# Sending the inverse RMS to all partitions through DRAM instead of through TensorE

## What is computed

```python
def _rmsnorm(x):
    return x * jax.lax.rsqrt(jnp.mean(x * x, axis=-1, keepdims=True) + EPS)

def _ada_rmsnorm(x, t, gamma_w, beta_w):
    gamma = (t @ gamma_w.T)[:, None, :]
    beta = (t @ beta_w.T)[:, None, :]
    return gamma * _rmsnorm(x) + beta

x = _L0_cond_ref(...)      # conditioned layer norm
x = x + a_alpha * _attention(_ada_rmsnorm(x, t, attn_gamma_w, attn_beta_w), W_q, W_k, W_v, W_o)
return x + f_alpha * _swiglu(_ada_rmsnorm(x, t, ffn_gamma_w, ffn_beta_w), gate_w, hidden_w, out_w, out_b)
```

## Time and profile before

| | |
|---|---|
| median of 3 runs | 1015.37 us (1011.99 to 1016.5) |
| profiled execution, its own time | 1012.19 us |
| span of its profile | 1010.4 us |
| busy PE / DVE / ACT / POOL | 964.5 / 691.4 / 625.8 / 565.9 us |
| granted TensorE clock, mean | 0.995 of full speed |

### The profile page before, as it was taken

How to read it: one execution, slowest core, us unless ns; L and a number is a source line. 1 busy time by engine, 2 the same in 40 slices (tenths; PEclk the granted TensorE clock), 3 DMA queues, 4 the chain that set the end, 5 groups by cost and what they waited for, 6 DMA issues and landing times.

```text
span 1010.4 us, 28503 instructions
## 1 busy us (share of the span) xinstructions
PE 964.5 (95%) x11164; PEld 900.0 (89%) x11164; DVE 691.4 (68%) x1347; ACT 625.8 (62%) x1775; POOL 565.9 (56%) x532
## 2 busy tenths in 40 slices
PE   5576999999999999999999999999999999999997
PEld 4455999999999999999999999999999999998897
DVE  6677676676777667677766767776777676666564
ACT  4556666667666666666666666666666666665432
POOL 4476646566564656656465665656565574443321
PEclk9899999999999999999999999999999999999999
DMA  6100001010100101010010101000000000000000
GB/s 209 43 22 22 2 12 33 12 33 2 33 13 12 33 12 33 2 33 12 12 33 13 32 2 34 12 13 32 13 25 9 13 12 13 12 13 12 12 12 21
DMA packets 20916, 23.36 MB, mean 23 GB/s; under 512 B 1200, under 2 KB 20272, under 8 KB 20784
## 3 DMA queue, kind: packets, MB, share of 16 engines
q1 hardware_dynamic: 20784, 21.54, 6.5%
HBM read 13.15 MB, written 8.39 MB: 21 GB/s over the span
## 4 chain that ended last, share of the span: by engine, by line
PE 86%; DVE 5%; issue 4%; ACT 3%; POOL 1%; DMA 0%; POOLq 0%; SPq 0%; ACTq 0%; DVEq 0%
PE psum L283 17%; PE psum L285 16%; PE psum L284 16%; PE psum L475 6%; PE psum L474 6%; PE psum L473 5%; PE psum L409 5%; PE psum L398 4%; PE psum L420 4%; PE psum L332 2%; PE psum L313 2%; ACT probs L826 2%; PE psum L321 1%; DVE least L585 1%; PE psum L469 1%
## 5 line engine op out<-in xcount | busy, mean ns | idle before, releaser
L283 PE MATMUL psum<-xf_hi,ffn_hi 128*128 128x256 f32 x1024 | 287.5, 281 | 4.2 <-DVE normed_f L633 1.6
L285 PE MATMUL psum<-xf_hi,ffn_lo 128*128 128x256 f32 x1024 | 285.9, 279 | 0.0
L284 PE MATMUL psum<-xf_lo,ffn_hi 128*128 128x256 f32 x1024 | 285.8, 279 | 0.0
L826 ACT ACTIVATE probs<-psum,least 128x64 f32<-128x64 f32 x976 | 213.0, 331 | 53.5 <-DVE least L585 30.0
L656 DVE SCALAR_TENSOR_TENSOR late<-tanh,psum 128x512 f32<-128x512 f32 x128 | 88.0, 687 | 188.7 <-ACT tanh L849 188.7
L283 PEld LDWEIGHTS psum<-xf_hi,ffn_hi 128*128 128x128 f32 x1024 | 192.2, 188 | 5.7 <-issue 4.4
L855 ACT ACTIVATE prod_hi<-late 128x512 fp32r<-128x512 f32 x128 | 80.7, 631 | 187.9 <-DVE late L664 129.0
L285 PEld LDWEIGHTS psum<-xf_hi,ffn_lo 128*128 128x128 f32 x1024 | 192.4, 188 | 0.0
L284 PEld LDWEIGHTS psum<-xf_lo,ffn_hi 128*128 128x128 f32 x1024 | 191.8, 187 | 0.0
L1006 POOL TENSOR_TENSOR probs<-probs,inv_sum 128x512 f32<-128x512 f32 x128 | 139.7, 1091 | 76.7 <-DVE inv_sum L606 76.2
L475 PE MATMUL psum<-prod_hi,ffn_lo 128*128 128x256 f32 x512 | 143.6, 281 | 0.0
(11 more groups left out here) (103 smaller groups left out, 2215.6 us busy)
## 6 DMA issues: line engine op xcount, KB each, us to landing
out_t_dram<-x_res SPq DMA_DIRECT2D x32, 256.0 KB, 2.1
xin<-x_dram SPq DMA_DIRECT2D x15, 512.0 KB, 3.9
w_raw<-attn_w_dram SPq DMA_DIRECT2D x1, 1024.0 KB, 7.0
x_res<-gate_w_dram SPq DMA_DIRECT2D x1, 1024.0 KB, 9.7
late<-hidden_w_dram SPq DMA_DIRECT2D x1, 1024.0 KB, 11.7
x_res<-out_w_dram SPq DMA_DIRECT2D x1, 1024.0 KB, 5.6
xin<-x_dram SPq DMA_DIRECT2D x2, 256.0 KB, 2.9
k_heads<-mod_w_dram SPq DMA_DIRECT2D x1, 320.0 KB, 4.6
```

Source lines behind the costliest of these rows:

```text
L283: pe.matmul(out, stat_hi, mov_hi, start=first, stop=False)
L284: pe.matmul(out, stat_hi, mov_lo, start=False, stop=False)
L285: return pe.matmul(out, stat_lo, mov_hi, start=False, stop=last)
L826: op = act.activation(probs[g % 2][:, h * SEQ:(h + 1) * SEQ], scores[:, h // 2, h % 2], ACT.Exp, bias=least[g % 2][:, h:h + 1], scale=-1.0)
```

## The change

The numbers `mean_sq` no longer go through TensorE in rounds with `grp >= 0`. SP writes them to a small DRAM tensor after GpSimd's power (second slot) and reads them back with the same row going to all 128 partitions, into `w_raw`, a tile that has served its time by then. The order of tokens in the transposes of the sums is changed so that the DRAM row is in token order. DVE's two scaling steps read `w_raw` (SBUF) where they read `norm_bank` (PSUM), and stand after `product` of the third slot. GpSimd's two beta steps move from the third slot into the fourth. ACT's two high parts move from before the exponentials of the fourth slot to between them and `half_tanh`. `ffn_split_lo` moves behind `product` of the fourth slot.

```diff
+        inv_dram = nc.dram_tensor("inv_dram", [2, 2 * PART], F32).ap()
+        inverse = [w_raw[:, i * 2 * PART:(i + 1) * 2 * PART] for i in range(2)]
...
+            def spread_inverses(grp):
+                which = slice(0 if is_part(grp + 2) else 1, 2 if is_part(grp - 2) else 1)
+                sp.wait_ge(inv_made, grp + 3)
+                sp.dma_start(inv_dram[grp % 2].rearrange("(w p i) -> p w i", w=2, i=2)[:, which],
+                             mean_sq[:].rearrange("p (w i) -> p w i", i=2)[:, which]).then_inc(inv_stored, 16)
...
+                sp.wait_ge(inv_stored, 16 * (grp + 1))
+                cols = slice(which.start * PART, which.stop * PART)
+                sp.dma_start(inverse[grp % 2][:, cols], inv_dram[grp % 2:grp % 2 + 1, cols].partition_broadcast(P)
+                             ).then_inc(spread_loaded, 16)
...
+                if s % PSEQ == 1 and s >= 0 and is_group(s // PSEQ):
+                    spread_inverses(s // PSEQ)
...
-                if norm_step(s) == 2 and is_group(grp) and s >= -4:
+                if norm_step(s) == 2 and -4 <= s < 0:
                     spread_inverses(grp)
...
-            def scale_by_rms(normed, first):
-                return dve.tensor_tensor(normed[:], normed[:],
-                                         norm_bank[:, first:first + PART].unsqueeze(1).broadcast_to([P, KT, PART]),
+            def scale_by_rms(normed, inverses):
+                return dve.tensor_tensor(normed[:], normed[:], inverses.unsqueeze(1).broadcast_to([P, KT, PART]),
                                          ALU.mult)
...
             def scale_f(m):
-                dve.wait_ge(inv_spread, m + 5)
                 dve.wait_ge(gamma_f, m + 1)
-                scale_by_rms(normed_f, PART).then_inc(scaled_f, 1)
+                dve.wait_ge(spread_loaded, 16 * (m + 3))
+                scale_by_rms(normed_f, inverse[m % 2][:, PART:2 * PART]).then_inc(scaled_f, 1)
```

More of the change, by code:

```diff
@@ L195, in norm_cols, with token_cols @@
             return slice(0 if is_part(grp + 2) else 2 * n, 4 * n if is_part(grp - 2) else 2 * n)
+        def token_cols(grp, ap, i):
+            return ap[:].rearrange("p (t i) -> p i t", i=2)[:, i] if grp >= 0 else ap[:, i * P:(i + 1) * P]
         def part_mod(row, m):
@@ L298, in norm_bank_read @@
                     pe.wait_ge(ms_read, grp + 3)
-                if j == 2 and is_part(grp + 2):
+                if j == 2 and grp < 0:
                     pe.wait_ge(scaled_a, grp + 3)
-                if j == 2 and is_part(grp - 2):
-                    pe.wait_ge(scaled_f, grp - 1)
             def norm_bank_free(s):
@@ L329, in spread_inverses @@
                 pe.wait_ge(inv_made, grp + 3)
-                cols = norm_cols(grp, 1)
-                for i in range(cols.start, cols.stop):
+                for i in range(2):
                     mm = pe.transpose(norm_bank[:, i * P:(i + 1) * P], mean_sq[:, i:i + 1].broadcast_to([P, P]),
@@ L623, in mean_squares_out @@
                 dve.wait_ge(ms_mm, grp + 3)
-                if grp >= -1:
+                if grp >= 1:
+                    dve.wait_ge(inv_stored, 16 * grp)
+                elif grp >= -1:
                     dve.wait_ge(inv_spread, grp + 2)
@@ L721, in _ @@
                     mean_squares_out(grp)
-                if norm_step(s) == 2 and is_part(grp + 2):
+                if norm_step(s) == 2 and s < 0:
                     scale_a(grp + 2)
@@ L753, in _ @@
                     product(f)
+                if j == 2 and s >= 0 and is_part(grp + 2):
+                    scale_a(grp + 2)
+                if j == 2 and is_part(grp - 2):
+                    scale_f(grp - 2)
+                if j == 3 and is_part(grp - 2):
+                    ffn_split_lo(grp - 2)
                 if grp % 2 == 0 and 2 <= (grp + 4) // 2 < NBLK:
@@ L900, in _ @@
                     attended_hi(grp - 1)
-                if j == 3 and is_part(grp + 2) and s != -1:
+                if s == FIRST_SLOT + 3:
                     split_hi_a(grp + 2)
-                if j == 3 and is_part(grp - 2):
-                    split_hi_f(grp - 2)
                 if s == FIRST_SLOT + 3:
@@ L911, in _ @@
                     exponentials(s)
+                if j == 3 and s >= 0 and is_part(grp + 2):
+                    split_hi_a(grp + 2)
+                if j == 3 and is_part(grp - 2):
+                    split_hi_f(grp - 2)
                 if is_step(f):
@@ L1038, in _ @@
                     inverse_rms(grp)
[L1039 removed]
+                if norm_step(s) == 2 and s < 0 or j == 3 and s >= 0 and is_part(grp + 2):
+                    apply_beta_a(grp + 2)
+                if j == 3 and is_part(grp - 2):
                     apply_beta_f(grp - 2)
[L1041 to L1042 removed]
                 if j == 3 and is_part(grp + 2) and s != -1:
```

23 lines of the change are left out of this document (15 added, 8 removed).

## The result

| | before | changed |
|---|---|---|
| median | 1013.9 us (4 runs, with one beside the changed kernel) | 1119.0 us (1118.3 to 1119.5, 4 runs) |
| ratio | 1 | 1.103, 95% interval 1.100 to 1.105 |
| span of the profile | 1010.4 us | 1116.9 us |

The kernel is slower by 105 us. I had forecast slower, but by 63 us; 1119 lies above the range of 1038 to 1106.

A forecast was written before the change was run, and what follows sets the result against it. TensorE sets the pace, with VectorE and ScalarE's chain close behind. Added 1.76 + 0.38 + 2.60 + 1.1 = 5.84 us less 1.16 slack gives 4.68 in two rounds, 63 us in 27 rounds: 1078 us, range 1038 to 1106.

The forecast's parts named there:

- What bounds the kernel: Steady rounds: TensorE sets the pace, but the chain of VectorE and ScalarE is nearly as long, with 0.58 us slack a round.
- TensorE's 0.41 a round: Third slot, scores to projection: dropping four spreading transposes saves TensorE 0.41 us a round, 11.1 us in 27 rounds.
- The slack of 1.16 in two rounds: Chain's waits for TensorE in second and third slots: 0.18 + 0.62 + 2 x 0.18 = 1.16 us in two rounds.
- The high parts, +1.05: Fourth slot: ScalarE's two high parts between exponentials and tanh, 0.53 us each, lengthen the chain by 1.05 us.
- In odd rounds I let VectorE's `product_lo` follow at 530.24: +0.91: After the third slot's product in odd rounds: `product_lo` directly follows the second scaling, ahead of GpSimd's beta step, costing 0.91 us.
- My figure for even rounds, 2.60: Third slot's product to fourth's tanh, even rounds: 1.75 - 0.20 + 1.05 = 2.60 us, with GpSimd getting in before `product_lo`.
- GpSimd gets in between VectorE's instructions everywhere: Rival, chance 0.20: odd rounds also pay 2.60, fourth slot's `product_lo` 1.28; 6.42 us in two rounds, 1102 us in all.
- order alone was put at 1.27: No-port rival, chance 0.18: third slot's product to fourth's tanh in odd rounds costs 0.42 - 0.20 + 1.05 = 1.27 us.
- `xf_lo` behind the fourth product: Fourth slot: `xf_lo` between product and `product_lo` waits for GpSimd, adding 0.38 us in odd rounds and 1.1 in even ones.
- 4.68 in two rounds: Steady rounds: added chain time of 5.84 us less 1.16 slack gives 4.68 us in two rounds, 2.34 a round.
- "I take 0" for the fill: Fill before round 3 and tail: taken as 0 us because of idle time, with -1 and +9 as ends.
- The DMA: Write to DRAM and read back: 2.1 us a leg, some 5 us with issue, hidden under about 10.8 us, cost 0.

## Why the prediction was wrong

- **What bounds the kernel**: right. The chain of VectorE and ScalarE runs close behind TensorE, and TensorE waited for `activate` as described. The runs bear it out from both sides: in the changed kernel each step taken off the chain paid, in the kernel before a step taken off the chain left its steady rounds as they were, and with the chain back in the old order two rounds came down to 58.5, what TensorE's own work asks for.
- **TensorE's 0.41 a round**: about 0.3. The spreading was priced rightly; the other part of the change, the transposes that read in steps of two, takes 0.12 back and had no term. In the changed kernel neither shows, since TensorE waits.
- **The slack of 1.16 in two rounds**: 0.97. The second slots gave their waits back and a little more (0.27 + 0.70). The two waits of 0.18 for the scores in the third slots stayed (the third slot's step is 8.04 as before); that TensorE starts its second slot late as well, and the scores with it, is my reading of this.
- **The high parts, +1.05**: right, 1.04 by the run that moved them.
- **The scaling and the port, "In odd rounds I let VectorE's `product_lo` follow at 530.24: +0.91"**: this is the step that failed. GpSimd's beta step, issued 0.45 us earlier, went first in every round, so odd rounds paid what I had given to even ones alone: 9.19 - 6.61 = 2.58 instead of 1.76. My figure for even rounds, 2.60, measured 2.58. It was the rival "GpSimd gets in between VectorE's instructions everywhere", to which I gave 0.20. The Trainium skill's rule on the port (SBUF — State Buffer, Who interferes with whom) says so: whoever issues first gets it, and the other waits. The rows above agree (`product_lo`, issued at 592.12, behind the beta step of 591.67). I had its order of issue from my own rows and weighed it too low. The runs with GpSimd's steps cut show that the waits are its: without beta the step of odd rounds fell from 9.19 to 8.35, and without beta and probabilities to 7.87, 1.26 over the kernel before, where order alone was put at 1.27.
- **`xf_lo` behind the fourth product**: +0.38 measured 1.22, again because GpSimd went first, and close to the rival's 1.28; +1.1 in even rounds measured 1.59, of it 0.6 order as forecast (8.78 in the run without beta and probabilities, 8.19 in the kernel before); the 0.5 too much is below, under what I had not expected.
- **Steady rounds**: 4.68 in two rounds was forecast, 7.0 measured. The rival's 6.42 lacks the 0.5 of even rounds and the 0.2 of slack that didn't come back, so its 1102 is too low as well.
- **"I take 0" for the fill**: 11 us, 8.7 of them from the change, at my upper end for fill and tail of 9; the tail's 2 come on top. The run from round 3 on gives them back. Engines with idle time were no cover. That each norm step is waited for by the next slots there is my explanation; no run takes the fill apart.
- **The DMA**: hidden, though 3.0 and 3.9 us a leg and not 2.1.

Summed in us: forecast 63, of it 31 order and 32 port. By the profiles 106.5: 60 port and 33 order in the steady rounds, 11 fill (8.7 by the change, the rest with the clock), 2 tail. So order was priced rightly, and port and fill are what was missed.

## What to carry to other kernels

A busy engine at 95% is the bound only by as much as the next chain is shorter; measure that difference from the waits of the chain for the bound engine, before taking work off the one or adding to the other. Moving work to a place "at the end of the slot" is free only if the engine has a wait there: here the wait for the tanh was free, and the place between product and low part was the chain. When an operand moves from PSUM to SBUF on VectorE, look at what GpSimd runs at that moment, and let the order of issue decide who waits.

## What I had not expected of the hardware

A VectorE instruction with one tile of 128 x 4 waits for GpSimd too. In the changed kernel, at the end of VectorE's list for the fourth slot of an even round, its scaling of the mean, and GpSimd's sum of squares for the first slot:

```profile
568.04 0.71 DVE L566 TENSOR_SCALAR mean<-merge 128x4 f32<-128x4 f32 x1
...
568.00 0.73 POOL L990 TENSOR_TENSOR square_sum_f<-squares_f 128x256 f32<-128x256 f32 x1 [1.22 <-ACT squares_f L802]
```

It takes 0.17 in the steady rounds of the kernel before and 0.71 here, in every even round with a merge, ending with GpSimd's instruction. That is the 0.5 us that even rounds paid beyond my sum; without beta and probabilities it is 0.17 again, and the 0.5 is gone. This one has a single SBUF input. My sentence that such an instruction does not contend left out an exception of the same section of the Trainium skill (SBUF — State Buffer, Who interferes with whom): it says so only of instructions outside the 2-port perf modes, and counts `tensor_scalar` among those that can enter one. The wait here agrees with that; in which mode the instruction ran, the trace does not show.

The two DMA legs took 3.0 us for 2 KB written in pieces of 8 bytes and 3.9 us for 256 KB read from one row. A store of 256 KB that had landed in 2.1 took 4.3 (median of 32) when it was issued right behind that load, and 2.1 again in the version where it waited for the scaling.
